# Moving two groups of transposes from TensorE to the DMA queues in a fused attention and 8-bit FFN kernel, with a third PSUM bank and a second normalisation in half tiles

## Chip, cores and metric

One Trainium2 chip, 8 cores. Every core runs the same program on its own 1024 of the 8192 tokens; there is no traffic between cores. The metric is the time of the slowest core in device microseconds (us).

## The reference

One pre-normalised transformer layer on x of [1, 8192, 2048], float32:

```
x = x + attn(layernorm(x))
x = x + ffn(layernorm(x))

attn: qkv = x @ w_qkv.T -> [B, N, 3, H=16, hd=128]
      att = softmax(einsum('bnid,bnjd->bnij', q, k) * hd**-0.5)
      out = einsum('bnij,bnjd->bnid', att, v)
      return out.transpose(0, 2, 1, 3).reshape(B, N, D) @ w_proj.T
ffn:  y = fake_quant(x, rows) @ fake_quant(kernel, columns) + fake_quant(bias)
      return fake_quant(relu(y), rows)
fake_quant(x): s = amax(|x|)/127;  clip(round(x / s), -127, 127) * s
```

The attention is between the 16 heads of one token (a 16x16 matrix per token), not between tokens. The transpose and reshape then mix heads and tokens, so that a core's output rows are not its input rows.

## The kernel before, in words

TensorE multiplies in bfloat16; weights arrive as float32 and are converted by the DMA (GpSimd's queue). All order is written out by hand: each engine has one instruction stream, semaphores join them, and an engine that waits holds up all that stands behind it in its stream. SP issues most DMAs and is such a stream too.

**Head.** SP loads the eight x tiles (128 tokens x 2048, 1 MB each). GpSimd loads six tiles of w_qkv (`wqb`), tile e after x tile e. VectorE takes statistics (`stats`), ScalarE normalises (`norm`, L319), TensorE transposes (`a_transpose`, L705), both copy out of PSUM.

**Projection** (`q_part`, L718). 48 weight tiles e times two token halves h are 96 jobs of 16 matmuls 128x512, in the order `JOBS`: the first `HEADE` = 5 tiles with h = 0, then the same with h = 1, then tiles with both, at last six tiles with h = 0 and the same six with h = 1 (`TAILE`). `NQ` = 90 jobs lie ahead of the attention slots. `q_evac` copies the results to qT, kT and vT, VectorE (L465) for even jobs and ScalarE (L333) for odd ones. Beside the jobs, every three of them from job 10, one tile `ft` of the FFN weights (`wkf`, rows of the transposed kernel) is rounded: `k_scale` (VectorE, absolute maximum, L489), `k_round` (ScalarE, L337), `k_quant` (VectorE, L498, to `kqr`); TensorE transposes it (`k_transpose`, 16 transposes, L736), `k_evac` copies it out (L506 VectorE, L345 ScalarE, into `kqt`), and SP stores it to `kq_spill` in HBM (L229).

**Slots.** From there on the program counts slots `sl`. Slot `sl` has, on TensorE: scores of group `sl` of 32 tokens x 16 heads (L753 adds the mask, L754 multiplies q and k), then 16 matmuls in two halves, and between and behind them `v_transpose(sl-1)` (L766), `a_transp(sl-1)` (L775) and `av(sl-2)` (L787). The 16 matmuls are the last six projection jobs in slots 0 to 5, then 32 of the output projection (`p_part`, L805, tile b and quarter u in slot 6 + 4b + u), then the FFN (`y_part`, L828, from slot 38 on). There are 32 groups, so the attention ends with slot 33. VectorE in slot `sl`: `row_max` (L511, and L516 that scales the maxima for the exponent), `p_evac` of the slot before (L539 adds the residual, L542 statistics), `v8_evac` (L523), `a_norm` (L527, L532). ScalarE: `st_evac` (L367), `exps` (L353), `att_evac` (L363). The output projection alternates between two PSUM banks.

**Second normalisation.** Every four slots from slot 11 one tile b: ScalarE subtracts the mean from the whole tile (`l_center`, L373), VectorE takes the absolute maximum (`l_scale`, L553), ScalarE scales and rounds (`l_round`, L383), VectorE writes `qx` (`l_quant`, L565), and SP transposes qx by DMA to xqT (`l_transpose`, L244). Two buffers `zb` alternate.

**SP in the slots** issues residual loads (`xres_load`, L238), normalisation transposes, the first quarter of the rounded weights back from HBM (`kq[0]`, L251) when all projection jobs are done, and quarters 1 to 3 (L262), 2 MB each, when jobs 28 + u of the output projection are done, since they overwrite the projection weights. The FFN's results are evicted (L575), scaled, rounded, clamped (L588), added (L594) and stored.

The release of quarter 1 in the code:

```
for u in range(1, 4):
    sync.wait_ge(S_("pMM"), 28 + u)
    inc(sync.dma_start(kq[u][:, :], d_kq[128 * u:128 * (u + 1), :]),
        f"kqL{u}", 16)
```

Of the kernel before, what the change touches and what calls it, by code (L numbers as in the profile page):

```python
# [19 lines left out]
MAGIC = 12582912.0  # L20

NW = 6
HEADE = 5
# [28 lines left out]
def build_program():  # L52
# [10 lines left out]
    d_out = nc.dram_tensor("out", [NL, D], F32, kind="ExternalOutput").ap()  # L63
    d_kq = nc.dram_tensor("kq_spill", [512, 8192], BF16).ap()
# [4 lines left out]
    def A(name, shape, dt, offset):  # L69
# [7 lines left out]
             offset=(131072 + 16384 * u) if u < 3 else 0) for u in range(4)]  # L77
# [6 lines left out]
    V8 = [A(f"V8{i}", [128, 512], BF16, offset=208896 + 1024 * i)  # L84
          for i in range(2)]
# [13 lines left out]
    kqt = [A(f"kqt{i}", [128, 2048], BF16, offset=122880 + 4096 * i)  # L99
           for i in range(2)]  # L100
# [7 lines left out]
    zb = [A(f"zb{i}", [128, 2048], F32, offset=180224 + 8192 * i)  # L108
          for i in range(2)]
    qx = A("qx", [128, 2048], BF16, offset=196608)  # L110
    bqb = A("bqb", [128, 2048], F32, offset=202752)
    tt = [A(f"tt{i}", [128, 2048], F32, offset=8192 * i) for i in range(2)]
# [13 lines left out]
    C_NBX = [172, 176]  # L126
# [6 lines left out]
    C_SC = [236 + t for t in range(8)]  # L133
# [8 lines left out]
    pF = [nc.alloc_psum_tensor(f"pF{i}", [128, 512], F32) for i in range(5)]  # L142
    pH = [nc.alloc_psum_tensor(f"pH{i}", [128, 1024], BF16) for i in range(3)]
# [15 lines left out]
    def wt(eng, handle):  # L159
        eng.wait_ge(S_(handle[0]), handle[1])  # L160

# [30 lines left out]
    def wait_half_evac(eng, i, semV, semS):  # L192

        if i % 2 == 0:
            eng.wait_ge(S_(semV), i // 2 + 1)
        else:
            eng.wait_ge(S_(semS), i // 2 + 1)

    with nc.Block() as blk:

        @blk.sync
        def _(sync):
# [16 lines left out]
            for ft in range(NC):  # L219
                if ft + 2 < NC:  # L220
                    sync.wait_ge(S_("kQ"), ft + 1)
# [4 lines left out]
                sync.wait_ge(S_("kEvV"), ft + 1)  # L226
                sync.wait_ge(S_("kEvS"), ft + 1)
                u, f4 = ft // 4, ft % 4
                inc(sync.dma_start(  # L229
                    d_kq[128 * u:128 * (u + 1), 2048 * f4:2048 * (f4 + 1)],  # L230
                    kqt[ft % 2][:, :]), f"kSt{ft % 2}", 16)

            sync.wait_ge(S_("kSt0"), 128)
            sync.wait_ge(S_("kSt1"), 128)
# [7 lines left out]
            def l_transpose(b):  # L242
                sync.wait_ge(S_("lQ"), b + 1)
# [4 lines left out]
            xres_load(0)  # L248
            xres_load(1)
            sync.wait_ge(S_("qMM"), NJ)  # L250
            inc(sync.dma_start(kq[0][:, :], d_kq[0:128, :]), "kqL0", 16)  # L251
            xres_load(2)
            for b in range(5):
                l_transpose(b)
                xres_load(b + 3)
            l_transpose(5)
            sync.wait_ge(S_("tO"), NG)
            inc(sync.dma_start(bqb[:, :], d_bq.partition_broadcast(128)),
                "bqL", 16)
            for u in range(1, 4):  # L260
# [677 lines left out]
```

## Time and profile before

| | |
|---|---|
| median of 3 runs | 683.57 us (682.66 to 684.41) |
| the profiled execution | 680.61 us |
| its span, slowest core | 679.1 us (cores 673.8 to 679.1) |
| TensorE matmul busy | 618.6 us, 91% |
| VectorE busy | 351.4 us, 52% |
| ScalarE busy | 235.7 us, 35% |
| DMA engines moved | 99.29 MB, 146 GB/s |

The profile is one execution, taken by the hardware profiler. Busy shares are averages over stages with different limits, so stretches are looked at one by one. "Idle before" of an instruction is the time its engine stood still ahead of it, and the arrow names what ended it. PE is TensorE, DVE VectorE, ACT ScalarE, POOL GpSimd, SPq the queue of SP. A matmul's own duration (380 ns) is longer than its place in the row (215 ns), as matmuls overlap.

### The profile page before, as it was taken

To read this page: it belongs to the slowest core of one execution; us is meant where nothing else is said; L and a number is where in the kernel's file an instruction comes from. 1 tells how busy PE (TensorE), PEld (TensorE's weight loads), DVE (VectorE), ACT (ScalarE), POOL (GpSimd) and SP (SyncE) were. 2 spreads that over 40 slices of the span, in tenths; PEclk is the share of its full clock that TensorE was granted. 3 is DMA by queue.
4 is the path that set the end of the run, shared out by engine and by line. 5 is a ranking of instruction groups with operands and counts; after the bars stand their busy time and mean duration, and the time that the engine had idled before them with its cause. 6 is when DMAs were issued, how large, how long until landed. Compare 5 with 4: busy or idle time off the path is not lost.

```text
span 679.1 us, 10007 instructions; the slowest of 8 cores (673.8 to 679.1 us)
## 1 busy us (share of the span) xinstructions
PE 618.6 (91%) x3545; PEld 313.3 (46%) x3600; DVE 351.4 (52%) x554; ACT 235.7 (35%) x485; POOL 34.6 (5%) x68
## 2 busy tenths in 40 slices
PE   1399999999999999999999999989898898999993
PEld 0244445445454544444444555555454443444442
DVE  3563446444644451100102567888878763666657
ACT  3663134233423341000011666567575622111111
POOL 0000100000000001111001000000000000000000
PEclk9999999999999999999999999989999998999997
DMA  8984999999999989999831615322313495112213
GB/s 229 256 204 144 160 218 192 208 221 215 197 203 225 208 163 170 175 157 156 151 63 29 97 62 187 94 73 86 91 35 94 120 340 129 62 63 84 103 63 124
DMA packets 37474, 99.29 MB, mean 146 GB/s; under 512 B 18993, under 2 KB 18993, under 8 KB 33585
## 3 DMA queue, kind: packets, MB, share of 16 engines
q1 hardware_dynamic: 28210, 65.09, 31.8%
q0 software_dynamic: 9216, 33.56, 30.8%
q8 instruction: 30, 0.49, 0.3%
q14 instruction: 18, 0.15, 0.1%
HBM read 111.21 MB, written 16.79 MB: 188 GB/s over the span
## 4 chain that ended last, share of the span: by engine, by line
PE 70%; DMA 9%; DVE 8%; ACT 7%; issue 4%; SPq 1%; DVEq 0%; ACTq 0%
PE pF L718 47%; PE pF L828 15%; DMA xbuf<-x_att 6%; PE pF L805 5%; ACT Ebuf L353 3%; DMA kq<-kq_spill 3%; PE pH L736 2%; DVE cols L553 2%; ACT zb L373 2%; DVE cols L511 2%; ACT zb L383 1%; DVE qx L565 1%; ACT aTT L363 1%; DVE xr L539 1%; SPq L204 1%
## 5 line engine op out<-in xcount | busy, mean ns | idle before, releaser
L718 PE MATMUL pF<-aT,wqb 128*128 128x512 bf16 x1501 | 332.8, 380 | 3.5 <-ACT aT L325 1.7
L718 PEld LDWEIGHTS pF<-aT,wqb 128*128 128x128 bf16 x1536 | 149.4, 98 | 176.3 <-issue 3.5
L805 PE MATMUL pF<-wpq,qT 128*128 128x512 bf16 x492 | 117.1, 382 | 11.2 <-DVE xr L539 10.2
L828 PE MATMUL pF<-kq,xqT 128*128 128x512 bf16 x496 | 109.2, 383 | 3.9 <-DMA kq<-kq_spill 2.6
L828 PEld LDWEIGHTS pF<-kq,xqT 128*128 128x128 bf16 x496 | 48.8, 99 | 64.4 <-issue 7.5
L805 PEld LDWEIGHTS pF<-wpq,qT 128*128 128x128 bf16 x512 | 47.9, 98 | 58.5 <-issue 11.8
L353 ACT ACTIVATE Ebuf<-pF,cols 128x128 bf16<-128x128 f32 x128 | 45.5, 372 | 48.6 <-DVE cols L516 48.6
L465 DVE CAST vT<-pF 128x512 bf16<-128x512 f32 x16 | 11.1, 691 | 80.8 <-PE pF L718 80.8
L465 DVE CAST kT<-pF 128x512 bf16<-128x512 f32 x16 | 11.1, 691 | 65.1 <-PE pF L718 65.1
L388 ACT ACTIVATE tt<-tt,cols 128x2048 f32<-128x2048 f32 x7 | 14.0, 2002 | 84.1 <-DVE cols L471 84.1
L575 DVE SCALAR_TENSOR_TENSOR tt<-pF,cols,bqb 128x512 f32<-128x512 f32 x31 | 23.3, 751 | 37.6 <-PE pF L828 37.6
L282 POOL DMA_DIRECT2D wqb<-wqkv x48 | 26.0, 541 | 314.7 <-PE pF L718 281.4
L333 ACT CAST vT<-pF 128x512 bf16<-128x512 f32 x16 | 9.4, 587 | 83.0 <-PE pF L718 83.0
L465 DVE CAST qT<-pF 128x512 bf16<-128x512 f32 x16 | 11.0, 690 | 52.4 <-PE pF L718 52.4
L333 ACT CAST kT<-pF 128x512 bf16<-128x512 f32 x16 | 9.4, 586 | 80.1 <-PE pF L718 80.1
L705 PE MATMUL pH<-ident,abuf 128*128 128x128 bf16 x128 | 11.7, 264 | 27.7 <-ACT abuf L319 27.7
L489 DVE TENSOR_REDUCE cols<-wkf 128x1 f32<-128x2048 f32 x16 | 36.4, 2277 | 0.0
L333 ACT CAST qT<-pF 128x512 bf16<-128x512 f32 x16 | 9.3, 587 | 71.4 <-PE pF L718 71.4
L337 ACT ACTIVATE wkf<-wkf,cols 128x2048 f32<-128x2048 f32 x16 | 32.1, 2004 | 5.4 <-DVE cols L471 5.4
L445 DVE BATCH_NORM_STATS2 cols<-xbuf 128x6 f32<-128x512 f32 x32 | 19.8, 681 | 16.6 <-DMA xbuf<-x_att 16.6
L511 DVE TENSOR_REDUCE cols<-pF 128x4 f32<-128x512 f32 x32 | 22.0, 687 | 12.2 <-PE pF L754 12.1
L353 ACT ACTIVATION_READ_ACCUMULATOR Ebuf<-pF,cols 128x1 f32 x128 | 26.8, 209 | 0.0
(70 smaller groups left out, 539.6 us busy)
## 6 DMA issues: line engine op xcount, KB each, us to landing
wqb<-wqkv POOLq DMA_DIRECT2D x48, 512.0 KB, 8.4
wkf<-wkT SPq DMA_DIRECT2D x16, 1024.0 KB, 8.9
xbuf<-x_att SPq DMA_DIRECT2D x8, 1024.0 KB, 23.0
kq_spill<-kqt SPq DMA_DIRECT2D x16, 512.0 KB, 6.9
wpq<-wp POOLq DMA_DIRECT2D x16, 512.0 KB, 11.4
xr<-x_res SPq DMA_DIRECT2D x8, 1024.0 KB, 6.2
kq<-kq_spill SPq DMA_DIRECT2D x4, 2048.0 KB, 14.3
out<-xr SPq DMA_DIRECT2D x7, 1024.0 KB, 4.7
```

The lines of the kernel that those rows point to most:

```text
L282: inc(g.dma_start(wqb[e % NW][:, :], d_wqkv[128 * e:128 * (e + 1), :]), f"wL{e % NW}", 16)
L333: inc(s.copy(qkv_dst(e, h), qkv_src(j)), "qEvS")
L337: inc(s.activation(wkf[ft % 2][:, :], wkf[ft % 2][:, :], AF.Copy, bias=MAGIC, scale=cc(C_KR[ft])), "kZ")
L353: i = s.activation(Ebuf[g % 2][:, cs], pF[3 + g % 2][:, cs], AF.Exp, bias=cc(C_NBX[g % 2] + j), scale=SCALE, accum_out=cc(C_DEN[g % 2] + j))
L445: h = inc(v.bn_stats(cc(c0 + 6 * q4, 6), xbuf[t][:, 512 * q4:512 * (q4 + 1)]), "vS")
L465: inc(v.tensor_copy(qkv_dst(e, h), qkv_src(j)), "qEvV")
L489: h = inc(v.reduce_max(cc(C_KA[ft % 2]), wkf[ft % 2][:, :], AX.X, apply_absolute_value=True), "vS")
L511: h = inc(v.tensor_reduce(cc(C_NM[g % 2], 4), pF[3 + g % 2].rearrange("p (j n) -> p j n", j=4), AX.X, ALU.max, negate=True), "vS")
L575: return inc(v.scalar_tensor_tensor(tt[k % 2][:, cs], pF[(4 * k + u) % 4][:, :], cc(C_SX[k]), bqb[:, cs], ALU.mult, ALU.add), "yEv")
L718: mm = tn.matmul(pF[QBANK[j]][:, :], wqb[e % NW][:, 128 * c:128 * (c + 1)], aT[:, 8192 * h + 512 * c: 8192 * h + 512 * (c + 1)], start=(c ...
L805: mm = tn.matmul(pF[f % 2][:, :], sT[:, 2048 * b + 128 * m: 2048 * b + 128 * (m + 1)], wpq[u][:, 512 * m:512 * (m + 1)], start=(m == 0), s ...
L828: mm = tn.matmul(pF[y % 4][:, :], xqT[:, 2048 * k + 128 * c: 2048 * k + 128 * (c + 1)], w[:, c, :, :], start=(c == 0), stop=(c == NC - 1))
```

## The change

The rounded FFN weight tiles are stored to HBM as rows (`kr_spill`), straight from `kqr`. TensorE's `k_transpose`, the two `k_evac` and `kqt` go. During the slots SP reads the tiles back by DMA transpose: tiles 0 to 3 into kq[0]; tiles 4 to 15 one after the other into one buffer `kst`, from which GpSimd stores each to `kq_spill`, and the next transpose waits for that store. The values are transposed by SP's DMA, eight tiles vT to V8, instead of TensorE's 32 groups with VectorE's copies. The attention transposes alternate between two PSUM banks; the output projection and the last projection jobs use three banks instead of two. The softmax scale is multiplied into q at its eviction, and the instruction that scaled the row maxima goes. The second normalisation works on half tiles, spread over six slots a tile, with one `zb`. The first six w_qkv loads wait for x tiles 2, 4, 6 and 7; `HEADE` is 4. The last projection weight quarter is loaded tile by tile. SP's order in the slots is written out anew. Buffers move. The diff, cut to its core:

```diff
-HEADE = 5
+HEADE = 4
...
+L0, LP = P0 + 5, 6
+SLOTB = (0, 1, 5)
...
 def _qbank(j):
     if j >= NQ:
-        return (j - NQ) % 2
+        return SLOTB[(j - NQ) % 3]
...
+    V8 = [A(f"V8{i}", [128, 2048], BF16, offset=4096 * i) for i in range(2)]
+    zb = A("zb", [128, 2048], F32, offset=8192)
+    kst = A("kst", [128, 2048], BF16, offset=200704)
+    qx = A("qx", [128, 2048], BF16, offset=196608)
+    bqb = A("bqb", [128, 2048], F32, offset=0)
+    tt = [A(f"tt{i}", [128, 2048], F32, offset=180224 + 8192 * i)
           for i in range(2)]
-    qx = A("qx", [128, 2048], BF16, offset=196608)
...
+                inc(sync.dma_start(d_kr[128 * ft:128 * (ft + 1), :],
+                                   kqr[ft % 2][:, :]), f"kSp{ft % 2}", 16)
...
+            def v_transpose(b):
+                if b == 0:
+                    sync.wait_ge(S_("qEvV"), NQ // 2)
+                    sync.wait_ge(S_("qEvS"), NQ // 2)
+                elif b == 4:
+                    sync.wait_ge(S_("qEvV"), NJ // 2)
+                    sync.wait_ge(S_("qEvS"), NJ // 2)
+                if b >= 2:
+                    sync.wait_ge(S_("tO"), 4 * b - 4)
+                inc(sync.dma_start_transpose(
+                    V8[b % 2].rearrange("p (c n) -> p c n", c=NC),
+                    vT[:, 2048 * b:2048 * (b + 1)]), f"vT{b}", 16)
+
             def xres_load(b):
                 sync.wait_ge(S_("tS"), 4 * b + 4)
-                sync.wait_ge(S_("tV"), 4 * b + 4)
+                sync.wait_ge(S_(f"vT{b}"), 16)
...
             def l_transpose(b):
-                sync.wait_ge(S_("lQ"), b + 1)
+                sync.wait_ge(S_("lQ"), 2 * b + 2)
...
+            def k_transpose(ft):
+
+
+                if ft < 4:
+                    sync.wait_ge(S_("qMM"), NJ)
+                    inc(sync.dma_start_transpose(
+                        kq[0][:, 2048 * ft:2048 * (ft + 1)].rearrange(
+                            "p (c n) -> p c n", c=NC),
+                        d_kr[128 * ft:128 * (ft + 1), :]), "kqL0", 16)
+                else:
+                    if ft == 4:
+                        sync.wait_ge(S_("qMM"), NJ)
+                    else:
+                        sync.wait_ge(S_("kSt"), 16 * (ft - 4))
+                    inc(sync.dma_start_transpose(
+                        kst.rearrange("p (c n) -> p c n", c=NC),
+                        d_kr[128 * ft:128 * (ft + 1), :]), "kT", 16)
+
+            def kq_load(u):
                 sync.wait_ge(S_("pMM"), 28 + u)
+                if u == 1:
+                    sync.wait_ge(S_("kSt"), 16 * 12)
                 inc(sync.dma_start(kq[u][:, :], d_kq[128 * u:128 * (u + 1), :]),
                     f"kqL{u}", 16)
-            l_transpose(6)
-            l_transpose(7)
-            for k in range(NT - 1):
+
...
+            v_transpose(0)
+            v_transpose(1)
+            xres_load(0)
+            v_transpose(2)
+            k_transpose(0)
+            k_transpose(1)
+            xres_load(1)
+            k_transpose(2)
+            k_transpose(3)
+            v_transpose(3)
+            k_transpose(4)
+            xres_load(2)
+            k_transpose(5)
+            v_transpose(4)
+            k_transpose(6)
+            xres_load(3)
+            k_transpose(7)
+            v_transpose(5)
+            l_transpose(0)
+            k_transpose(8)
+            xres_load(4)
+            k_transpose(9)
+            v_transpose(6)
+            k_transpose(10)
+            xres_load(5)
+            l_transpose(1)
+            k_transpose(11)
+            v_transpose(7)
+            k_transpose(12)
+            xres_load(6)
+            k_transpose(13)
+            l_transpose(2)
+            k_transpose(14)
+            xres_load(7)
+            k_transpose(15)
+            sync.wait_ge(S_("tO"), NG)
+            inc(sync.dma_start(bqb[:, :], d_bq.partition_broadcast(128)),
+                "bqL", 16)
+            kq_load(1)
+            l_transpose(3)
+            kq_load(2)
+            kq_load(3)
+            l_transpose(4)
+            out_store(0)
+            l_transpose(5)
+            out_store(1)
+            l_transpose(6)
+            out_store(2)
+            out_store(3)
+            l_transpose(7)
+            for k in range(4, NT - 1):
+                out_store(k)
...
-                if e < NW:
-                    g.wait_ge(S_(f"xL{e}"), 16)
+                if e < 3:
+                    g.wait_ge(S_(f"xL{2 * e + 2}"), 16)
+                elif e == 3:
+                    g.wait_ge(S_("xL7"), 16)
                 if e >= NW:
                     g.wait_ge(S_("qMM"), JIDX[(e - NW, 1)] + 1)
                 wq_load(e)
                 if 33 <= e < 45:
                     wp_load((e - 33) // 4, (e - 33) % 4)
-            g.wait_ge(S_("qMM"), NQ)
             for i in range(4):
+                g.wait_ge(S_("qMM"), JIDX[(NE - TAILE + i, 1)] + 1)
                 wp_load(3, i)
+            for ft in range(4, NC):
+                u, f4 = ft // 4, ft % 4
+                g.wait_ge(S_("kT"), 16 * (ft - 3))
+                inc(g.dma_start(
+                    d_kq[128 * u:128 * (u + 1), 2048 * f4:2048 * (f4 + 1)],
+                    kst[:, :]), "kSt", 16)
...
-                                     AF.Exp, bias=cc(C_NBX[g % 2] + j),
-                                     scale=SCALE,
+                                     AF.Exp, bias=cc(C_NM[g % 2] + j),
...
+            def l_center(b, h):
+                cs = slice(1024 * h, 1024 * (h + 1))
+                if h == 0:
+                    s.wait_ge(S_("lMu"), b + 1)
+                    if b >= 1:
+                        s.wait_ge(S_("lQ"), 2 * b)
+                inc(s.activation(zb[:, cs], xr_half(b, h), AF.Identity,
                                  bias=cc(C_NMU[b])), "lC")
...
+                b, r = (sl - L0) // LP, (sl - L0) % LP
+                if 0 <= b < NT:
+                    if r < 2:
+                        l_center(b, r)
+                    if r == 0:
+                        l_rstd(b)
+                    if 3 <= r < 5:
+                        l_round(b, r - 3)
...
+                if e < 16:
+                    inc(v.tensor_scalar(qkv_dst(e, h), qkv_src(j), SCALE, None,
+                                        ALU.mult), "qEvV")
...
             def row_max(g):
                 v.wait_ge(S_("tS"), g + 1)
-                h = inc(v.tensor_reduce(
+                inc(v.tensor_reduce(
                     cc(C_NM[g % 2], 4),
                     pF[3 + g % 2].rearrange("p (j n) -> p j n", j=4), AX.X,
-                    ALU.max, negate=True), "vS")
-                wt(v, h)
-                inc(v.tensor_scalar(cc(C_NBX[g % 2], 4), cc(C_NM[g % 2], 4),
-                                    SCALE, None, ALU.mult), "vMx")
-
-            def v8_evac(g):
-                v.wait_ge(S_("tV"), g + 1)
-                if g >= 2:
-                    v.wait_ge(S_("tO"), g - 1)
-                inc(v.tensor_copy(V8[g % 2][:, :], pH[0][:, 0:512]), "vV8")
+                    ALU.max, negate=True), "vMx")
...
+                b, r = (sl - L0) // LP, (sl - L0) % LP
+                if 0 <= b < NT:
+                    if r == 1:
+                        h_l0 = l_max(b, 0)
+                    elif r == 2:
+                        l_scale(b, h_l0, l_max(b, 1))
+                    elif r >= 4:
+                        l_quant(b, r - 4)
...
                 tn.wait_ge(S_("sAT"), g + 1)
-                tn.wait_ge(S_("vV8"), g + 1)
+                if g % 4 == 0:
+                    tn.wait_ge(S_(f"vT{g // 4}"), 16)
                 if g >= 1:
...
-                        wait_job_evac(tn, NQ + f - 2)
+                    if f - 3 < P0:
+                        wait_job_evac(tn, NQ + f - 3)
                     else:
-                        tn.wait_ge(S_("pEv"), f - 2 - P0 + 1)
+                        tn.wait_ge(S_("pEv"), f - 3 - P0 + 1)
...
-                        tn.wait_ge(S_(f"kqL{u}"), 16)
+                        tn.wait_ge(S_(f"kqL{u}"), 64 if u == 0 else 16)
...
-                ft, ph = (j - PREP0) // 3, (j - PREP0) % 3
-                if ph == 0 and 0 <= ft - 1 < NC:
-                    k_transpose(ft - 1)
...
-                        v_transpose(sl - 1)
                         a_transp(sl - 1)
```

## Rows read from the trace of the kernel before

**Rows 1.** Spans and granted TensorE clock of the cores (1.0 is full speed), slowest core
```profile
core 0: 679.1 us, clock 0.990
```
**Rows 2.** Busy times by stretch: PE, PEld, DVE, ACT, POOL, clock, DMA share, GB/s
```profile
94.00:263.00 169.00, 168.16 (x947) 83.95 (x962) 79.15 (x95) 53.67 (x51) 12.66 (x24) 1.00 0.93 202
...
368.20:538.00 169.80, 156.47 (x1166) 90.12 (x1189) 128.63 (x260) 106.38 (x347) 1.80 (x4) 0.99 0.34 91
540.70:565.70 25.00, 21.06 (x96) 9.08 (x95) 14.44 (x22) 7.55 (x8) 0.00 (x0) 1.00 1.00 302
```
**Rows 3.** Chain of waits in the projection: start us, us, what (repeats 16 times)
```profile
113.10 0.89 PE pH L736 x16
114.05 10.31 PE pF L718 x47
124.35 0.89 PE pH L736 x16
```
**Rows 4.** Timeline of TensorE, slot 0 and slot 4: start us, us, engine, line
```profile
368.16 0.22 PE L753 MATMUL pF<-neg,ident 128*128 128x128 bf16 x1 [0.82 <-ACT vT L333]
...
385.55 0.22 PE L753 MATMUL pF<-neg,ident 128*128 128x128 bf16 x1
...
387.72 0.39 PE L766 MATMUL pH<-ident,vT 128*128 128x128 bf16 x4
387.94 0.39 PE L775 MATMUL pH<-ident,Ebuf 128*128 128x128 bf16 x4
...
390.12 0.22 PE L753 MATMUL pF<-neg,ident 128*128 128x128 bf16 x1
```
**Rows 5.** Timeline of all engines, one stall in the slots
```profile
444.58 2.29 DVE L553 TENSOR_REDUCE cols<-zb 128x1 f32<-128x2048 f32 x1 [1.41 <-ACT zb L373]
...
447.43 0.69 DVE L511 TENSOR_REDUCE cols<-pF 128x4 f32<-128x512 f32 x1
...
449.39 2.50 PE L805 MATMUL pF<-wpq,qT 128*128 128x512 bf16 x7 [2.23 <-DVE xr L539]
```
**Rows 6.** VectorE's groups from 395 to 538 us: busy, mean ns, idle before
```profile
L539 DVE TENSOR_TENSOR xr<-pF,xr 128x512 f32<-128x512 f32 x28 | 19.3, 691 | 0.3 <-PE pF L805 0.2
L542 DVE BATCH_NORM_STATS2 cols<-xr 128x6 f32<-128x512 f32 x27 | 18.7, 694 | 2.8
L532 DVE TENSOR_TENSOR Ebuf<-Ebuf,cols 128x512 bf16<-128x512 bf16 x26 | 18.0, 692 | 2.7
L511 DVE TENSOR_REDUCE cols<-pF 128x4 f32<-128x512 f32 x26 | 17.8, 686 | 4.6 <-PE pF L754 4.6
...
L523 DVE COPY V<-pH 128x512 bf16<-128x512 bf16 x27 | 11.1, 411 | 1.5 <-PE pH L766 1.1 <-issue 0.4
...
L516 DVE TENSOR_SCALAR cols<-cols 128x4 f32<-128x4 f32 x26 | 4.4, 169 | 2.8
```
**Rows 7.** Timelines of SP and of TensorE, reload of the FFN weights
```profile
540.85 7.22 SPq L262 DMA_DIRECT2D kq<-kq_spill  x3
...
565.75 4.44 PE L828 MATMUL pF<-kq,xqT 128*128 128x512 bf16 x12 [2.65 <-DMA kq<-kq_spill]
```
**Rows 8.** Timelines of VectorE and TensorE in the head
```profile
48.54 2.47 DVE L445 BATCH_NORM_STATS2 cols<-xbuf 128x6 f32<-128x512 f32 x4 [2.18 <-DMA xbuf<-x_att]
...
56.11 24.12 PE L718 MATMUL pF<-aT,wqb 128*128 128x512 bf16 x109
```
**Rows 9.** DMA issues: KB each, median us from issue to landing
```profile
wqb<-wqkv POOLq DMA_DIRECT2D x48, 512.0 KB, 8.4
...
xr<-x_res SPq DMA_DIRECT2D x8, 1024.0 KB, 6.2
...
out<-xr SPq DMA_DIRECT2D x7, 1024.0 KB, 4.7
...
out<-xr SPq DMA_DIRECT2D x4, 256.0 KB, 2.6
xqT<-qx SPq DMA_TRANSPOSE x8, 3.7
```

More of the change, by code:

```diff
@@ L76, in build_program @@
     wpq = [A(f"wpq{u}", [128, 8192], BF16,
-             offset=(131072 + 16384 * u) if u < 3 else 0) for u in range(4)]
+             offset=131072 + 16384 * u) for u in range(4)]
     wqb = [A(f"wqb{i}", [128, 2048], BF16, offset=180224 + 4096 * i)
@@ L125, in build_program @@
     C_NM = [164, 168]
-    C_NBX = [172, 176]
     C_DEN = [180, 184]
@@ L132, in build_program @@
     C_AM = [228 + t for t in range(8)]
-    C_SC = [236 + t for t in range(8)]
+    C_SC = [287 + t for t in range(8)]
     C_RR = [244 + t for t in range(8)]
@@ L140, in build_program @@
     C_NMG = 286
[L142 to L143 removed]
+    pF = [nc.alloc_psum_tensor(f"pF{i}", [128, 512], F32) for i in range(6)]
+    pH = [nc.alloc_psum_tensor(f"pH{i}", [128, 1024], BF16) for i in range(2)]
     sems, cnt = {}, {}
@@ L330, in q_evac @@
                 if e == 32:
-                    s.wait_ge(S_("kSt0"), 128)
-                    s.wait_ge(S_("kSt1"), 128)
-                inc(s.copy(qkv_dst(e, h), qkv_src(j)), "qEvS")
+                    s.wait_ge(S_("kSp0"), 128)
+                    s.wait_ge(S_("kSp1"), 128)
+                if e < 16:
+                    inc(s.activation(qkv_dst(e, h), qkv_src(j), AF.Copy,
+                                     scale=SCALE), "qEvS")
+                else:
+                    inc(s.copy(qkv_dst(e, h), qkv_src(j)), "qEvS")
             def k_round(ft):
@@ L362, in att_evac @@
                     s.wait_ge(S_("tO"), g - 1)
-                inc(s.copy(aTT[g % 2][:, :], pH[1][:, 0:512]), "sAT")
+                inc(s.copy(aTT[g % 2][:, :], pH[g % 2][:, 0:512]), "sAT")
             def st_evac(g):
@@ L408, in _ @@
                     k_round(ft)
-                if ph == 1 and 0 <= ft - 1 < NC:
-                    k_evac(ft - 1)
             for sl in range(NS + 2):
@@ L699, in a_transpose @@
                 for hb in range(2):
-                    i = 2 * t + hb
-                    if i >= 3:
-                        wait_half_evac(tn, i - 3, "aEvV", "aEvS")
+                    if t >= 1:
+                        tn.wait_ge(S_("aEvV" if hb == 0 else "aEvS"), t)
                     for j in range(8):
                         c = 8 * hb + j
-                        tr = tn.transpose(pH[i % 3][:, 128 * j:128 * (j + 1)],
+                        tr = tn.transpose(pH[hb][:, 128 * j:128 * (j + 1)],
                                           abuf[t % 4][:, 128 * c:128 * (c + 1)],
@@ L724, in q_part @@
                     inc(mm, "qMM")
-            def k_transpose(ft):
-                tn.wait_ge(S_("kQ"), ft + 1)
-                for hb in range(2):
-                    i = 16 + 2 * ft + hb
-                    if i - 3 < 16:
-                        wait_half_evac(tn, i - 3, "aEvV", "aEvS")
-                    else:
-                        wait_half_evac(tn, i - 19, "kEvV", "kEvS")
-                    for j in range(8):
-                        c = 8 * hb + j
-                        tr = tn.transpose(pH[i % 3][:, 128 * j:128 * (j + 1)],
-                                          kqr[ft % 2][:, 128 * c:128 * (c + 1)],
-                                          ident[:, :])
-                    inc(tr, "kT")
             def scores(g):
@@ L756, in scores @@
                 inc(mm, "tS")
[L758 to L768 removed]
             def a_transp(g):
                 tn.wait_ge(S_("vNm"), g + 1)
[L772 to L773 removed]
+                if g >= 2:
+                    tn.wait_ge(S_("sAT"), g - 1)
                 for j in range(4):
[L775 removed]
+                    tr = tn.transpose(pH[g % 2][:, 128 * j:128 * (j + 1)],
                                       Ebuf[g % 2][:, 128 * j:128 * (j + 1)],
```

143 lines of the change are left out of this document (42 added, 101 removed).

## The prediction

> **What bounds the kernel now.** I read the spans first: core 0 is the slowest, its granted clock is 0.990 of the upper level, 2.4 GHz, so no throttle needs explaining [rows 1]. The profiled execution took 680.6 us, 1.5 us around its span of 679.1; the three timed runs have their median at 683.57, 3.0 higher. I make the sum against 680.6 and add the 3.0 at its end. About 0.3% of the time, 2 us, is what a measurement of this kernel can tell from no change.
>
> Next the busy times by stretch. From 94 to 263 us TensorE is busy for 168.2 of 169 us, and the DMA engines at 0.93. In the attention stretch it is busy for 156.5 of 169.8, with VectorE at 128.6: here something else sets the pace part of the time [rows 2]. The chain of waits shows the first stretch as a strict rhythm: 10.31 us of projection matmuls, then 0.89 us of transposes of the rounded FFN weights, with a period of 124.35 - 113.10 = 11.25 us [rows 3]. The transposes stand in series with the matmuls.
>
> The timeline of TensorE gives the attention slot. Undisturbed, it lasts 390.12 - 385.55 = 4.57 us; the value transposes in it take 387.94 - 387.72 = 0.22 us. Slot 0 begins at 368.16 [rows 4] and slot 34 ends at 540.7, where the load of the second quarter of the FFN weights is released [rows 7]: 172.5 us for 35 slots, where 32 at 4.57 and three at about 3.7 would be 157. The 15 us between are a stall that returns every four slots: VectorE is held by the 2.29 us maximum over a whole tile of the second normalisation, so the row maximum comes late, and behind it in VectorE's order the eviction that frees one of two banks; TensorE waits 2.23 us [rows 5].
>
> **Part 1, the weight transposes off TensorE.** 16 tiles, each 11.25 - 10.31 = 0.94 us with its gaps: 15.0 us gone. ScalarE and VectorE lose their two copies per tile, which were hidden. The cover to lose is the DMA's: the same bytes pass in 10.35 us instead of 11.25, and 0.93 of busy time becomes 1.01 [rows 2], if busy shares scale so. Six weight buffers and five banks smooth this. Bounds: 0 and 0.1 x 16 = 1.6 us; I take 0, as the busy share rises with queueing and the bytes moved there (202 GB/s) are below those of the reload of the FFN weights (302) [rows 2]. **-15.0**
>
> **Part 2, the head.** GpSimd no longer lets a weight tile follow each x tile: the first three follow x tiles 2, 4 and 6, the other three tile 7. The last x tile reaches VectorE at 48.54 and the transposes of it end where the matmuls go on at 56.11 [rows 8]. Three of six weight loads leave its way. But the job order has four, not five, first jobs, and each now waits for a later weight tile. Bounds +2 and -6 us; I take **-2**, since a tile's arrival is exchanged for another's.
>
> **Part 3, the slots.** Without value transposes a slot is 4.57 - 0.22 = 4.35 us. The scale moves into the evictions of q, which adds no instruction and takes the 0.17 us one away behind each row maximum [rows 6]. Will VectorE keep up? Each slot: row maximum 0.686, eviction 0.691, statistics 0.694, normalising 0.692 and its reciprocal (0.18, estimate) = 2.94 us; the V copy (0.411) goes. The tile's mean 0.1, and the second normalisation, now spread over six slots: its maximum of 2.29 [rows 5], the subtraction (1.2, estimate) and five small ones, 4.3/6 = 0.7; with about 0.3 of gaps between dependent instructions 4.1 of 4.35 [rows 6]. The heaviest slot (half a maximum, 1.14, and the scale's four small ones) has about 5.4, 1.05 too much, and the next has no piece and gives it back. The chain scores, maximum, exps, normalising takes about 4.3 us from the slot's start and is due after 6.1, so 1.05 is carried; and with a third bank the eviction has a slot more. So the stall goes, except for some 2 us: 32 slots at 4.35, less 0.7 for parts that the first two lack, three more at 3.67 (3.45 of projection and what is left of the attention), together 149.5; + 2 = 151.5. **-21.0**
>
> **Part 4, the price: the queues of DMAs.** SP now issues eight value transposes, 16 weight transposes, eight residual loads and three normalisation transposes in one order, each behind its wait. A value tile is issued at the end of slot 4b-3 and used in slot 4b+2: 21 us, hidden. A residual tile is issued in slot 4b+3 and used in 4b+7. What isn't hidden is the relay of twelve tiles through one buffer (kst): transpose from HBM, landing, GpSimd's store, landing, next transpose, SP standing still meanwhile. It begins when v_transpose(3) is out, about 45 us after slot 0's start (slot 9 ends at 43), and the second weight quarter may not be loaded before its end. One round:
> - transpose: the same size from SBUF lands in 3.7 us; a load of 1 MB from HBM in 6.2. Near the first, plus an HBM read: 4.2.
> - store of 512 KB: between 256 KB (2.6) and 1 MB (4.7) by SP, linearly 3.3; from GpSimd with its conversion of type 8.4 in a busy stretch. Near the first: 4.0.
> - handing over: 0.3.
> - other traffic beside the relay: six residual and seven half-size tiles, 10 MB, at 302 GB/s 33 us, of which I let 40% fall on it: 1.1 [rows 2, 9].
>
> A round is 9.6 us (bounds: 3.7 + 3.3 + 0.2 = 7.2, and 6.2 + 8.4 + 0.3 = 14.9), twelve are 115, and they end at 45 + 115.2 = 160.2, where the load was due at 151.5. What stands behind SP's waits is late too, but inside its cover: the last residual tile is issued behind the transpose of tile 14, at 45 + 10 x 9.6 = 141, lands by 147 and is used at 151.5. GpSimd has nothing else to do by then. **+8.7**, one for one: before, three loads released within 7.2 us already left TensorE waiting 2.65 us for the last [rows 7]. And l_transpose(3) now stands between the loads, half a megabyte: **+2.1**.
>
> **Part 5, the last stage.** The halves of tiles 4 to 7 now run beside the FFN matmuls: VectorE gets 0.7 us a slot more, where eviction, maximum, clamp and addition take some 2.2 of 3.45 (an estimate from the durations of the same sizes, [rows 5, 6]). Four banks cover the peaks: 0, bounds 0 and 4. The tail is untouched.
>
> **Sum.** 680.6 - 15.0 - 2.0 - 21.0 + 8.7 + 2.1 = 653.4; on the scale of the median 656.4.
>
> **The rivals.**
> - *The relay is hidden.* A round of 8.9 us or less ends by 151.5. For it: the DMA share of the attention stretch was 0.34 [rows 2]; transposes land in 3.7. Time 656.4 - 8.7 = 647.7; with a better head 643. Chance 0.30.
> - *VectorE stays the bound.* It is filled to 94%, and gaps may be wider than I allow. Slots of 4.8 us from slot 6 on: 26 x 0.45 = 12 us back, 163.5 in all, which also hides the relay: 656.4 - 8.7 + 12 = 659.7. The stretch showed VectorE waiting for others for a good part [rows 5], which speaks against it. Chance 0.12.
> - *The relay is long.* Rounds of 10.6 to 11.9 us, because the queue is fuller: 58 us of DMA time in the stretch before (0.34 x 169.8), and 24 transposes at 2 and 12 stores at 1.7 more, makes some 125 of 151 us. Time 668 to 683. Chance 0.10.
> - *Slower: the relay eats everything.* From a round of 11.9 us on (36 us gained otherwise, over twelve rounds 3.0 each, on top of 8.9) the kernel is slower. Place: SP's wait for the kst store, and TensorE's wait for the second quarter. With 13 us: 45 + 156 - 151.5 = 49.5 instead of 8.7, 697; with 14.9, 720. For it: GpSimd's loads needed 8.4 [rows 9], and no row shows a transpose out of HBM. Chance 0.10.
>
> By the Trainium skill, VectorE: DVE Perf Modes, section "The three transpose paths", TensorE needs 390 ns for a block of 128x128 and the DMA path 1309, which speaks against this change: sixteen blocks one behind the other would be 20.9 us (an estimate from that page), a round some 26, and the kernel near 860 us. The trace does not agree: a tile of sixteen blocks lands in 3.7 us [rows 9]; that it held for a source in HBM is 0.02 of the last rival's 0.10.
>
> My own case (rounds of 8.9 to 10.6 us, 648 to 668) has 0.38.
>
> **The numbers.** Time 656.4. Range 642 to 679: from the hidden relay with a good head to most of the long relay; left out are the slower case and a sliver of the others. Faster by more than 0.3%: 0.30 + 0.12 + 0.38 + 0.08 of the long relay = 0.88; within: 0.02; slower: 0.10.
>
> **What would show it.** Right: the group of weight transposes on TensorE is gone and the projection has no gap from 56 to its end, slot 0 about 351; scores 4.35 us apart, no waits of over 1 us for the xr eviction; the twelve stores of kst about 9.6 us apart; TensorE waits about 13 us in all for kq (2.65 before). Wrong: stores less than 8.9 apart and a wait of 3 to 5 us (hidden); scores 4.8 apart with VectorE without idle time (bound by VectorE); waits of TensorE for value tiles or residual tiles, which I cost at nothing, since 17 us cover each; waits for weight tiles between 94 and 263 us, which would break part 1.

## The result and the profile after

| | before | after |
|---|---|---|
| median (in the comparison) | 683.12 us (4 runs) | 673.25 us (4 runs, 669.90 to 674.34) |
| ratio of after to before | | 0.9846, 95% interval 0.9807 to 0.9886 |
| profiled execution | 680.61 us | 673.67 us |
| span, slowest core | 679.1 us | 672.1 us |
| spans of the cores | 673.8 to 679.1 | 661.4 to 672.1 |

Faster by 1.5%, where 3.9% (656.4 us) was forecast. The cores, which had run within 5 us of each other, now spread over 11. Executions in which one die ran several per cent longer at a lower granted clock (one of run 6, two of run 8 and some of the kernel before) are left out of every median and ratio below.

The part of the page that tells the chain of waits. In the kernel before, TensorE made 70% of the chain and DMA 9%; now two DMAs of the relay stand in it that did not exist before:

```profile
PE 64%; DMA 27%; SPq 5%; issue 2%; DVE 1%; ACT 0%; DVEq 0%; POOLq 0%; ACTq 0%
PE pF L790 48%; PE pF L876 15%; DMA kst<-kr_spill 10%; DMA kq_spill<-kst 9%; DMA xbuf<-x_att 5%; SPq L261 2%; DMA kq<-kq_spill 2%; SPq L252 1%; DMA wqb<-wqkv 1%; SPq L239 1%; SPq L203 1%; PE pF L810 0%; DVE xr L765 0%; PE pF L811 0%; DVEq L198 0%
```

The chain in order of time (start us, us, what) shows the projection without a break, then rounds of the relay one after the other, and the load that waited for them:

```profile
51.34 297.16 PE pF L790 x1376
...
349.31 0.22 PE pF L810
...
394.81 6.15 DMA kst<-kr_spill
401.00 0.52 issue
401.51 5.87 DMA kq_spill<-kst
407.44 6.87 DMA kst<-kr_spill
414.36 0.51 issue
414.87 3.84 DMA kq_spill<-kst
418.77 4.63 DMA kst<-kr_spill
...
529.83 5.42 DMA kq_spill<-kst
535.32 0.33 SPq L278
535.74 8.89 SPq L252
544.72 10.44 DMA kq<-kq_spill
```

The first line answers to [rows 3]: no transposes between the matmuls. No weight tile is late there either, though the DMA share is 0.97 where it was 0.93 [rows 2]:

```profile
94.00:263.00 169.00, 169.00 (x785) 76.60 (x783) 68.73 (x81) 41.43 (x38) 15.31 (x30) 1.00 0.97 216
```

The relay begins at 394.81 and ends at 535.3: twelve rounds in 140.5 us, 11.7 us each. Shares of the span with one more digit are 10.4% and 9.5%, so a round is 5.8 us of transpose, 5.3 of store and about 0.6 of handing over. On the eight cores of this execution a round takes 10.7 to 11.7 us, 11.1 in the mean.

TensorE's timeline around the reload, answering to [rows 7] (start us, us, engine, line; in brackets its idle time and what ended it):

```profile
531.06 5.30 PE L876 MATMUL pF<-kq,xqT 128*128 128x512 bf16 x16 [3.94 <-DVE xr L605]
544.92 5.69 PE L876 MATMUL pF<-kq,xqT 128*128 128x512 bf16 x16 [8.57 <-DMA kq<-kq_spill]
555.29 101.99 PE L876 MATMUL pF<-kq,xqT 128*128 128x512 bf16 x464 [4.68 <-DMA kq<-kq_spill]
```

TensorE waits 8.6 us for the second quarter and 4.7 for the third. Who waited for whom (us in total, times, longest) tells what else the relay held up: SP stood 73.8 us in it, and the residual loads behind it in SP's order came late.

```profile
DVE xr L605 <- DMA xr<-x_res: 24.5, 4, 7.5
...
DVE qx L639 <- DMA xqT<-qx: 13.7, 3, 9.4
PE pF L876 <- DMA kq<-kq_spill: 13.2, 2, 8.6
```

The same for SP's queue:

```profile
SPq L269 <- DMA kq_spill<-kst: 73.8, 11, 10.2
```

The busy times by stretch, with the columns of [rows 2]. Early in the slots TensorE has no gap; from 437 us on it does, and its granted clock falls there, to 0.82 and 0.77 of full speed around the long waits (means of its two levels, 2.4 and 1.2 GHz). The job of 16 matmuls behind the wait of 8.6 us took 5.69 us, one at full clock takes 3.61. The low clock came with the idling: in runs 1 and 3 below, without the relay, TensorE hardly waits from 437 to 498 us and runs at 1.00 there; run 1 waits for weights between 520 and 544 us, and there its clock is 0.57.

```profile
395.00:437.00 42.00, 42.00 (x312) 23.81 (x311) 33.69 (x64) 30.91 (x104) 1.61 (x3) 1.00 0.73 157
437.00:480.00 43.00, 35.99 (x261) 19.73 (x258) 27.57 (x56) 26.33 (x88) 2.13 (x4) 0.97 0.83 177
480.00:520.00 40.00, 34.45 (x192) 17.08 (x193) 21.45 (x40) 18.75 (x53) 1.63 (x4) 0.90 0.72 165
520.00:544.00 24.00, 11.77 (x46) 4.46 (x43) 9.27 (x17) 2.19 (x2) 1.02 (x2) 0.82 0.71 225
544.00:563.00 19.00, 13.39 (x44) 5.08 (x45) 2.80 (x4) 2.57 (x4) 0.00 (x0) 0.77 0.94 276
```

Laid beside the trace of before, stage by stage of the two profiled executions:

| stage | before | after | moved | forecast |
|---|---|---|---|---|
| start of the steady projection | 56.1 | 51.3 | -4.8 | -2.0 |
| from there to slot 0 | 312.1 | 298.0 | -14.1 | -15.0 |
| slot 0 to the load of the second quarter | 172.7 | 186.0 | +13.3 | -12.3 |
| from that load to the end | 138.2 | 136.8 | -1.4 | +2.1 |

One line is wrong by 25.6 us, the others by 0.9 to 3.5.

### The profile page after: what moved, and what is told of

It is laid out like the page before. It is cut to its first block, busy times and chain, and to the rows that moved or that the text cites. A ratio compares the mean times of both kernels' runs of the same rounds, so it can differ in the third digit from the quotient of the medians.

```text
span 672.1 us, 9055 instructions; the slowest of 8 cores (661.4 to 672.1 us)
## 1 busy us (share of the span) xinstructions
PE 605.8 (90%) x3216; PEld 292.9 (44%) x3216; DVE 324.7 (48%) x498; ACT 225.3 (34%) x485; POOL 41.0 (6%) x80
## 4 chain that ended last, share of the span: by engine, by line
PE 64%; DMA 27%; SPq 5%; issue 2%; DVE 1%; ACT 0%; DVEq 0%; POOLq 0%; ACTq 0%
PE pF L790 48%; PE pF L876 15%; DMA kst<-kr_spill 10%; DMA kq_spill<-kst 9%; DMA xbuf<-x_att 5%; SPq L261 2%; DMA kq<-kq_spill 2%; SPq L252 1%; DMA wqb<-wqkv 1%; SPq L239 1%; SPq L203 1%; PE pF L810 0%; DVE xr L765 0%; PE pF L811 0%; DVEq L198 0%
## 5 line engine op out<-in xcount | busy, mean ns | idle before, releaser
L790 PE MATMUL pF<-aT,wqb 128*128 128x512 bf16 x1536 | 336.3, 381 | 3.4 <-ACT aT L401 2.6
L876 PE MATMUL pF<-kq,xqT 128*128 128x512 bf16 x496 | 113.0, 392 | 17.2 <-DMA kq<-kq_spill 13.2
L853 PE MATMUL pF<-wpq,qT 128*128 128x512 bf16 x512 | 123.0, 386 | 0.6 <-DVE xr L605 0.6
L548 DVE CAST kT<-pF 128x512 bf16<-128x512 f32 x16 | 11.1, 692 | 63.0 <-PE pF L790 63.0
L545 DVE TENSOR_SCALAR qT<-pF 128x512 bf16<-128x512 f32 x16 | 11.0, 690 | 52.5 <-PE pF L790 52.5
L605 DVE TENSOR_TENSOR xr<-pF,xr 128x512 f32<-128x512 f32 x32 | 21.9, 684 | 25.3 <-DMA xr<-x_res 24.5
L410 ACT ACTIVATE qT<-pF 128x512 bf16<-128x512 f32 x16 | 9.5, 598 | 72.8 <-PE pF L790 72.8
L777 PE MATMUL pH<-ident,abuf 128*128 128x128 bf16 x128 | 11.7, 264 | 20.4 <-ACT abuf L395 20.4
L447 ACT ACTIVATE zb<-xr,cols 128x1024 f32<-128x1024 f32 x16 | 18.6, 1160 | 31.6 <-DVE qx L639 31.6
```

The lines of the kernel that those rows point to most:

```text
L548: inc(v.tensor_copy(qkv_dst(e, h), qkv_src(j)), "qEvV")
L605: h = inc(v.tensor_tensor(xq4, pF[SLOTB[(P0 + 4 * b + u) % 3]][:, :], xq4, ALU.add), "pEv")
L790: mm = tn.matmul(pF[QBANK[j]][:, :], wqb[e % NW][:, 128 * c:128 * (c + 1)], aT[:, 8192 * h + 512 * c: 8192 * h + 512 * (c + 1)], start=(c ...
L853: mm = tn.matmul(pF[SLOTB[f % 3]][:, :], sT[:, 2048 * b + 128 * m: 2048 * b + 128 * (m + 1)], wpq[u][:, 512 * m:512 * (m + 1)], start=(m = ...
L876: mm = tn.matmul(pF[y % 4][:, :], xqT[:, 2048 * k + 128 * c: 2048 * k + 128 * (c + 1)], w[:, c, :, :], start=(c == 0), stop=(c == NC - 1))
```

## The experiments

Medians are of three to five executions; each ratio is against the kernel before on the same chip. Runs 1 to 4, 5 to 8 and 9 to 11 ran on three chips, where the kernel before took 681.9, 682.1 and 681.5 us, against 683.1 beside the change; so differences in us across these groups are uncertain by 1 to 2 us. Line numbers shift a little from kernel to kernel.

### 1. No relay, tiles transposed straight into place

```diff
 def kq_load(u):
     sync.wait_ge(S_("pMM"), 28 + u)
-    if u == 1:
-        sync.wait_ge(S_("kSt"), 16 * 12)
-    inc(sync.dma_start(kq[u][:, :], d_kq[...]), f"kqL{u}", 16)
+    for f4 in range(4):
+        inc(sync.dma_start_transpose(kq[u][:, 2048 * f4:2048 * (f4 + 1)]...,
+            d_kr[128 * (4 * u + f4):...]), f"kqL{u}", 16)
-            k_transpose(4)
...
-            k_transpose(15)
```

> No relay: tiles 4 to 15 are not transposed into kst and stored, but transposed straight into kq[1..3] once the projection weights there are used up. Theory A (the relay's rounds are the loss: SP stands in them, residual loads come late, and the second quarter comes late): slots at 4.35 us with no wait for residual tiles, slot 34 ends about 151.5 us after slot 0; then twelve transposes at 2.9 us (two of kq[0] took 5.75 us to issue) need 35 us where TensorE gives 22.4, so it waits some 14 us for kq in all; 32 us lost now become 14: about 655 us. Theory B (the value transposes or VectorE hold the slots): the slots stay long and the time stays above 668.

Measured: 658.08 us, ratio 0.9645 (0.9628 to 0.9662). From 437 to 498 us, where the changed kernel waited, the slots of the slowest core have no gap at all, at 1.00 of the clock:

```profile
437.00:480.00 43.00, 43.00 (x319) 24.38 (x318) 34.49 (x68) 32.82 (x111) 0.00 (x0) 1.00 0.43 103
480.00:498.00 18.00, 18.00 (x112) 9.26 (x110) 14.52 (x28) 10.09 (x27) 0.00 (x0) 1.00 0.26 87
```

and SP's timeline shows the transposes behind it:

```profile
498.95 11.53 SPq L278 DMA_TRANSPOSE kq<-kr_spill  x4
510.57 2.59 SPq L252 DMA_TRANSPOSE xqT<-qx  x1
513.26 25.58 SPq L278 DMA_TRANSPOSE kq<-kr_spill  x8
```

Its waits (us in total, times, longest) tell what they cost TensorE:

```profile
PE pF L860 <- DMA kq<-kr_spill: 18.3, 2, 11.2
```

Slot 34 ends at 498.95, 149.7 us after slot 0 (349.25): Theory A stands, the value transposes and VectorE hold nothing (Theory B falls). A row of transposes from HBM takes 25.58 / 8 = 3.2 us a tile, not 2.9, hence a wait of 18.3 instead of 14 and 658 instead of 655.

### 2. The relay in half tiles

```diff
+for h in range(2):
+    if ft > 4: sync.wait_ge(S_(f"kSt{h}"), 16 * (ft - 4))
+    inc(sync.dma_start_transpose(kst[:, 1024 * h:1024 * (h + 1)]...,
+        d_kr[128 * ft:128 * (ft + 1), 1024 * h:1024 * (h + 1)]), f"kT{h}", 16)
```

(GpSimd stores each half when it has landed.)

> The relay in half tiles: kst is cut in two, each half transposed and stored on its own, so that one half's store runs beside the other's transpose; bytes, order and everything else as in the changed kernel. Theory A (a round is latency: 11.7 us of which only some 4.5 us are transfer): a tile takes about 8.7 us, the relay ends within slot 34, waits for residual tiles go, about 649 us. Theory C (the DMA engines are full, busy share 0.81 in the slots): the tile still takes 11 us or more and the time stays at 670 to 676.

Measured: 671.20 us, ratio 0.9844 (0.9815 to 0.9873), as the changed kernel. The relay still goes from 395.48 to 533.10, 11.5 us a tile on the slowest core (10.6 to 11.5 on the eight). SP's timeline:

```profile
407.03 2.65 SPq L271 DMA_TRANSPOSE kst<-kr_spill  x2
410.31 1.88 SPq L239 DMA_TRANSPOSE V<-vT  x1
415.99 3.42 SPq L271 DMA_TRANSPOSE kst<-kr_spill  x2
```

and the DMA issues (KB each, median us to landing):

```profile
kq_spill<-kst POOLq DMA_DIRECT2D x24, 256.0 KB, 5.1
...
kst<-kr_spill SPq DMA_TRANSPOSE x24, 4.9
```

Theory A is missed, and time and round are what theory C expected, but this is no proof for full DMA engines: both halves are issued in one go, land one shortly after the other, are stored and come back together, so one half's store hardly runs beside the other's transpose. Half a tile takes 4.9 and 5.1 us to land, nearly as long as a whole one. What that means was left open here and settled by run 11.

### 3. The weight transposes back on TensorE

`k_transpose`, `k_evac`, `kqt` and the plain reload of before return; values by DMA, three banks, scaled q, half tiles and head stay.

> Part 1 undone alone: the rounded weights are transposed by TensorE during the projection again, copied out and stored as quarters; no relay. Values by DMA, third bank, scaled q, half-tile normalisation and head stay. Theory A: the relay's loss of 27 us goes and 15 us of TensorE transposes come back: 661 us, slots at 4.35 us. Theory B: the slots stay at 4.8 us or more, 675 us or above.

Measured: 654.62 us, ratio 0.9604 (0.9589 to 0.9619): better than the whole change by 18.6 us. From slot 0 (364.7) to the release of the second quarter (514.4), in the columns of [rows 2]:

```profile
364.70:514.40 149.70, 148.54 (x1052) 83.51 (x1074) 105.92 (x201) 101.85 (x348) 2.11 (x4) 1.00 0.53 130
```

and its wait for the weights:

```profile
PE pF L875 <- DMA kq<-kq_spill: 2.7, 2, 2.6
```

35 slots take 149.7 us where they took 172.7, and the reload costs 2.7 us, as before the change. The relay is the whole loss. It was worth more than the 27 us that I had put on it: 18.6 + 15 = 33.6 (by the ratios, 16.5 + 15 = 31.5).

### 4. The normalisation transpose ahead of the loads

```diff
-            kq_load(1)
             l_transpose(3)
+            kq_load(1)
             kq_load(2)
```

> Only the normalisation transpose of tile 3 is moved ahead of the load of the second quarter, from between it and the third. Theory D (SP stood 8.9 us in issuing it behind a 2 MB load, and the third quarter was issued that much later): the 4.7 us that TensorE waited for the third quarter go, 668 to 669 us. Rival (the queue is served in order and the bytes are the same): no more than 1 us, 672 to 674 us.

Measured: 671.27 us, ratio 0.9859 (0.9800 to 0.9918); against 0.9846 it shows no gain. The transpose now stood behind another load, the broadcast of the bias:

```profile
522.80 0.54 SPq L323 DMA_DIRECT2D bqb<-bq_spill  x1
523.44 8.34 SPq L252 DMA_TRANSPOSE xqT<-qx  x1
537.08 1.27 SPq L278 DMA_DIRECT2D kq<-kq_spill  x3
```

The order of the loads did bring something: from the load of the second quarter to the end the slowest core took 132.5 us instead of 136.8 (132.3 instead of 137.3 in the mean of the eight). But the transpose now ran beside the relay's last store, which took twice as long as in the changed kernel (5.42 us, above; in the mean of the eight cores 9.8 against 5.4). In the chain of waits:

```profile
526.03 10.97 DMA kq_spill<-kst
```

From the last transpose of the relay to the load it was 16.6 us instead of 11.4 (15.5 instead of 10.6 in the mean of the eight cores). Theory D's 4 to 5 us were won in one place and lost in the other; run 9 asks again with a relay that ends before the loads.

### 5. A mixed version

Tiles 0 to 3 go straight into kq[0] as in the change, 4 to 11 over the relay, 12 to 15 are transposed by TensorE. SP's order is written so that the eight rounds spread over slots 10 to 31:

```diff
+NP = 12
...
+            if ft < NP:   spill kqr to kr_spill
+            else:         wait for k_evac, store kqt to kq_spill
...
+            v0 v1 x0 v2 k0 k1 x1 k2 k3 v3 k4 x2 k5 v4 x3 k6 v5 l0
+            k7 x4 k8 v6 x5 l1 k9 v7 k10 x6 l2 k11 x7
```

(v, x, k, l: value transpose, residual load, weight transpose, normalisation transpose.)

> A version meant to beat both: tiles 0 to 3 by DMA transpose straight into kq[0], tiles 4 to 11 over the relay (eight rounds instead of twelve, SP's order written out anew so that each residual load stands ahead of the round it would wait for), tiles 12 to 15 transposed by TensorE during the projection. Theory A (one round is 11.7 us and eight of them, 94 us from 45 us on, end at 139, before slot 34 ends at 151.5): nothing of the relay is seen, and against the kernel with all tiles on TensorE (654.6) twelve tiles at 0.94 us are saved: 643 to 646 us. Rival (SP standing in the rounds delays residual tiles whatever their number): waits of VectorE for xr in the slots, 650 us or more.

Measured: 645.04 us, ratio 0.9462 (0.9432 to 0.9492), within theory A. The profiled execution was the longest of the four, 648.6 us. On its slowest core a store took 8.0 us in the median and the load could be issued at 510.5 only, 8 us past the end of slot 34 (353.1 + 149.7); VectorE waited 4.8 us for residual tiles and TensorE 8.7 for the weights. So the rival had a part on that one core.

### 6. The value transposes back on TensorE

> The changed kernel with the value transposes back on TensorE, in slots of 4.57 us; the relay of twelve stays. Theory A (the relay's length sets the time, so that the slots' own length does not count): only the eight value transposes leave the queues, a round falls from 11.7 to about 11.2 us, 666 to 670 us although 7 us of TensorE work come back. Rival E (the value transposes between the rounds are what stretched them): rounds of 9.6 us or less, 655 us or less. Rival B (slots set the time): 680 us.

(TensorE's value transposes, VectorE's copies of them and the single bank of the attention transposes return; the relay stays as in the change.)

Measured: 675.42 us, ratio 0.9907 (0.9873 to 0.9940): above the 666 to 670 of theory A and below the 680 of rival B, so the time alone decides nothing, and the trace has to. On the slowest cores the relay began 3.9 us later, behind longer slots (398.7 instead of 394.8), and ended at 535.3 in both; that end, and not the slots, released the second quarter (Rival B falls). Rounds went from 11.7 to 11.4 us there, and from 11.1 to 10.9 in the mean of the eight cores. So the value transposes do not stretch the rounds (Rival E falls); I had expected 0.5 us a round from them, and it was 0.2 to 0.3, which the later start ate up.

### 7. The relay's transposes read SBUF

```diff
-                        d_kr[128 * ft:128 * (ft + 1), :]), "kT", 16)
+                        wpq[0][:, 0:2048]), "kT", 16)
```

> The twelve relay transposes read a tile in SBUF (a piece of the projection weights) instead of the rounded weights in HBM, so three quarters of the FFN weights are not what they should be; sizes, order and waits are as in the changed kernel. Theory F (the source in HBM makes a transpose land in 5.8 us, where value tiles from SBUF land in 4.8 in the same queue): 1.0 us less a round, rounds of 10.7, 660 to 663 us. Rival (contention with the other transfers makes the 5.8, not the source): under 0.3 us a round, 669 us or more.

Measured: 658.74 us, ratio 0.9655 (0.9634 to 0.9676). Its slowest core:

```profile
kq_spill<-kst POOLq DMA_DIRECT2D x12, 512.0 KB, 5.1
kst<-wpq SPq DMA_TRANSPOSE x12, 4.0
```

4.0 us instead of 5.8, in the same queue among the same kinds of transfers. Rounds take 10.0 us on this core (9.4 to 10.1 on the eight, 9.8 in the mean), 1.3 us less than with the source in HBM in the mean and 1.7 on the slowest cores; 1.0 was expected. The load of the second quarter goes out 18.1 us earlier on the slowest core, and that core ends 14.6 us earlier. With a round of 10.0 the prediction's own sum gives 656.4 + 12 x 0.4 = 661.2, 2.5 above the measured time; it runs high for longer rounds too (see below), so the nearness proves little. The source in HBM is most of what I had missed. Whether that is the read itself or the traffic of all cores at HBM, this run does not part.

### 8. Both transposes on TensorE

> The kernel with the weights on TensorE (654.6), with the value transposes there too: what is left of the change are the third bank, the scaled q, the half-tile normalisation and the head. Theory A (a slot costs 4.57 instead of 4.35 us and the stalls stay away): 654.6 + 32 x 0.22 = 662 us. Rival (VectorE, with 0.41 us a slot more, is full at 4.5 of 4.57 us and stalls come back): 666 us or more.

Measured: 663.49 us, ratio 0.9718 (0.9699 to 0.9736), 8.9 above run 3, of which 32 x 0.22 = 7.0 are the transposes. It lies between theory A (662) and the rival (666). Starts of the scores in it: 386.39, 390.96, 395.53, 400.10, each 4.57 us on. What is left of the change, without moving a single transpose to the DMA, is 18 us: by the forecast's terms the stall of [rows 5] and the head. Third bank, scaled q and half tiles were not tried one by one.

### 9. The mixed version with the normalisation transpose behind the loads

```diff
             kq_load(1)
-            l_transpose(3)
             kq_load(2)
             kq_load(3)
+            l_transpose(3)
```

> The mixed version (645.0) with the normalisation transpose of tile 3 behind the three loads of the FFN weights instead of between them. Theory D (SP stands some 9 us in issuing it behind a 2 MB load, and the third quarter is issued so much later): the 6.9 us that TensorE waited for the third quarter shrink to about 3, 640 to 642 us. Rival (bytes and queue are the same): 644 to 646 us.

Measured: 640.05 us (639.49 to 640.60), ratio 0.9391 (0.9377 to 0.9405), the best of all: 6.1% faster than the kernel before, 4.9% (33 us) faster than the change (4.6% by the ratios). Cores end within 3 us of each other. SP's timeline:

```profile
503.13 7.16 SPq L290 DMA_DIRECT2D kq<-kq_spill  x3
```

and TensorE's wait:

```profile
PE pF L920 <- DMA kq<-kq_spill: 1.1, 1, 1.1
```

All three loads are issued within 7.2 us, where the run before it (run 5) had the first at 510.51, then 8.59 us of SP in the transpose. 1.1 us of waiting are left of 8.7. Part of the 5 us is that no core's relay was late this time; the fastest core, which had no such trouble in either run, went from 637.8 to 635.0 us. So the order alone is worth some 3 us.

### 10. Six tiles each way

> As the run before it, and with six tiles on TensorE and six in the relay instead of four and eight. Theory A (in the mixed version the relay of the slowest core ended 509 us, some 5 us after slot 34): that core's 5 us are won and 2 x 0.94 us of TensorE paid, 2 to 3 us below the run before it. Rival (eight rounds are hidden on all cores that count): 2 us above it.

Measured: 641.91 us, ratio 0.9423 (0.9407 to 0.9439), 1.9 above run 9. That is the rival: two tiles more on TensorE, 2 x 0.94. Eight rounds are hidden: in run 9 the relay ends at 489.5 to 497.1 us on the eight cores, and the load goes out at 501.1 to 503.3.

### 11. Half the bytes in each round

```diff
-                        kst.rearrange("p (c n) -> p c n", c=NC),
-                        d_kr[128 * ft:128 * (ft + 1), :]), "kT", 16)
+                        kst[:, 0:1024].rearrange("p (c n) -> p c n", c=8),
+                        d_kr[128 * ft:128 * (ft + 1), 0:1024]), "kT", 16)
```

> The changed kernel with a relay that transposes and stores only the first half of each tile's columns, one half-size transfer at a time; the other half of quarters 1 to 3 is filled at the reload from the same first half, so the FFN weights are not what they should be. Theory L (a round is made of fixed times from issue to landing): it falls from 10.4 to 11.7 us on the cores by no more than 2, to 9 us or more, about 655 us. Theory G (a round is made of the transfers' bytes at the rate that the full queues leave them): it falls to 7 us or less, the relay is hidden, about 648 us.

Measured: 651.38 us, ratio 0.9553 (0.9537 to 0.9569). The chain of its slowest core:

```profile
406.88 4.04 DMA kst<-kr_spill
...
411.48 5.23 DMA kq_spill<-kst
416.77 3.66 DMA kst<-kr_spill
...
420.96 4.78 DMA kq_spill<-kst
425.80 3.87 DMA kst<-kr_spill
```

Rounds of 8.8 to 9.8 us with half the bytes, where whole tiles gave 10.7 to 11.7: 1.9 us less, on the slowest cores and in the mean. The time lies midway between the 655 of theory L and the 648 of theory G; the rounds decide for L, since G asked for 7 us or less. Drawn on in a straight line (an estimate), 7 to 8 of the 11 to 12 us of a round do not depend on its bytes, and a relay with one buffer pays them twelve times.

## Why the prediction was wrong

**What held.** The bound was where it was forecast: the relay through kst, from 45.5 us after slot 0 (forecast 45) to the load of the second quarter, which it held back to 186.0 us after slot 0, where 149.7 would have done (runs 1 and 3). That the end of the kernel follows one for one was nearly right: in run 7 the load is 18.1 us earlier and the slowest core ends 14.6 earlier. Part 1 gave -14.1 (forecast -15.0); no weight tile was late in the projection, though the DMA share rose from 0.93 to 0.97. Part 3 was right too, but can only be seen with the relay away: 149.7 us from slot 0 to that load in runs 1 and 3, where 151.5 was forecast; VectorE keeps up. The rule of the Trainium skill that speaks against DMA transposes (VectorE: DVE Perf Modes, "The three transpose paths", 1309 ns a block) would have made a round some 26 us (the prediction's estimate from that page); a tile of sixteen blocks took 5.8 us to land, even out of HBM, so the trace speaks against that price for tiles of this size.

**What failed** is one term of Part 4: "A round is 9.6 us". It was 11.7 on the slowest core (11.1 in the mean of the eight), 25 us over twelve rounds, and that is the 25.6 us of the third line of the table. By its parts: the transpose was taken at 4.2 us, "near the first, plus an HBM read", and took 5.8. Run 7 shows that the source in HBM makes 1.8 of it (medians of the slowest cores; 1.3 by the means of all eight). The store was taken at 4.0 and took 5.3; no run parts that excess into causes. The 1.1 us that I added for other traffic was no separate term, it is inside these landings: rounds shrink by 0.2 to 0.3 when the value transposes leave (run 6) and by 1.9 when half the relay's own bytes do (run 11). I had both ends of the range (3.7 and 6.2; 3.3 and 8.4) and chose near the lower end of each, and that choice decided, because a round counts twelve times; a round at the middle of both ranges, 11.1 with handing over, would have given 674, though that would have met the 673.3 partly by luck, since the sum runs 8 us high for the rounds as measured. "The relay is long" (rounds of 10.6 to 11.9, 668 to 683) was the case that came true, at a chance of 0.10; "the relay is hidden", at 0.30, deserved less than that.

**Smaller ones.** With 11.7 in the prediction's sum it would read 681.6, 8 more than measured. The head gave 2.8 more than forecast, the projection 0.9 less. The last stage took 1.4 us less instead of 2.1 more, though l_transpose(3) held SP for 8.9 us, more than the 2.1 counted for it. Before, TensorE last waited for the fourth quarter, which landed 24.8 us after the first of the three loads went out; after, it last waited for the third, which landed at 19.8, with one job of 3.4 us more still to do. The first load landed in 9.5 us and the third quarter in 10.4, where before the three took 12.5, 15.0 and 17.9. Why they land sooner is open: in run 3, with the same order and the cores in step, the first needs 9.1 to 10.8 us, so the cores' spread is not needed for it. And the 3.0 us added for the median did not apply: the median lies 0.4 below the profiled execution after. "Inside its cover" for what stands behind SP's waits was wrong: VectorE waited 24.5 us for residual tiles, the sign of being wrong that the prediction had "cost at nothing". It probably cost nothing of its own, as TensorE would have waited for the second quarter in any case (argued, not tried). It also makes a hit of the forecast luck: TensorE waits 13.2 us for kq, "about 13" was forecast, but the load came 25.8 us later than forecast, and by then TensorE had stood 17.1 us behind VectorE, whose own waits were those for residual tiles. What remains open is why one core's rounds take 11.7 us and another's 10.7 in the same execution, and so why the cores spread.

## What to carry to other kernels

A transfer that must land before the next may be issued is priced by its time from issue to landing more than by its bytes, and a chain of n such pairs through one buffer costs n times that; count the rounds, take the price from a row with the same source and the same company, and if there is none, state the bounds and do not choose near the lower end without a reason. When an engine's work is moved to a serial chain beside it, move only as many pieces as fit under its cover: eight tiles were free here, twelve cost some 33 us. In a queue whose issuing engine stands still while a transpose is issued behind a large load, put the loads first (some 3 us here).

## What was not expected of the hardware

- A DMA transpose of 128x2048 in bf16 lands (medians of the cores) in 3.7 us out of SBUF in the kernel before, 3.8 to 4.4 among the relay's transfers, and 4.7 to 5.8 out of HBM; back to back out of HBM one takes 3.2 us.
- Halving a transfer of 512 KB takes little off its time: from 5.8 to 4.1 us for the transpose, from 5.1 to 4.2 for GpSimd's store on the slowest cores.
- SP is held while it issues a DMA transpose behind a load: 8.9 us behind one of 2 MB, 8.3 behind one of 1 MB, against 1.6 with no load ahead. Plain loads of 2 MB were issued three in 7.2 us.
